# One graph layer on one core: the per-group sum of edge messages over two ranges of 16 nodes instead of one range of 32

## The chip, the core and the metric

The kernel runs on one core of a Trainium2 chip. The metric is the device time in microseconds, from one launch. PE is the matrix engine and PEld its loading of stationary operands, DVE the vector engine, ACT the scalar engine, POOL the engine that here issues the indirect gathers, and SP the engine that issues most other DMAs.

## What is computed

The layer takes 12,500 nodes of 160 features and 412,500 edges sorted by their target node `dst`. Cut to what matters:

```python
h = relu(layernorm(x))                       # 12500 x 160
l0, l1 = linear(h)                           # table of 160 columns, read by edge source
w = relu(edge_attr_10 @ W_fc1 * c) @ W_fc2   # 412500 x 192: w0 w1 (64 each), w2 w3 (32 each)
y0, y1 = l0[src], l1[src]
m0 = w0 * y0 * e0
m1 = (w1 * y0)[:, :, None] * e1[:, None, :]
m2 = (w2 * e0)[:, :, None] * y1
m3 = w3 * einsum('eud,ed->eu', y1, e1)       # times 1/sqrt(3)
s  = segment_sum(m, dst)                     # per node
out = x + second_linear(h, s)
```

The four edge attributes e0 and e1 multiply products of w and y, and the sum runs over all edges of a node.

## The kernel before

First the layer norm and the first linear map are computed for all nodes and written to DRAM as a table `T` (rows of 160 floats). Then the edge loop runs over NG = 538 groups `g` of six tiles `t` of 128 edges, and the last group has one tile. Each engine has its own program over all groups, and semaphores alone tie them together. A semaphore wait on an engine holds everything behind it on that engine.

For each group, by line of the kernel before:

- POOL (L525 to L533) gathers the 128 table rows of each tile into `Y`, with one `indirect_dma_start` per tile, six in a group. `Y` has NB = 4 buffers, so the gathers of group g + 4 wait until the last product of group g has been made (L527, semaphore `s_p`).
- PE `radial` (L662) makes the first edge layer, two matmuls of 384 columns into `bank[0]` and `bank[1]`. ACT `relu` (L586) moves it to `hs`. PE `weights(g, u)` (L672) makes w for the two tiles of unit u, with u = 0, 1, 2, into `bank[2]` or `bank[3]` in turn.
- DVE `windows` (L618 to L625) makes from the target numbers a table of zeros and ones `oh` over 32 nodes, and from it and the four edge attributes the stationary operand `S` (128 edges by 4 x 32 columns per tile). It also makes `Cm`, which shifts the previous group's sums. DVE `weigh(g, u)` (L633, L636) multiplies w with the gathered rows into `P`, two products s = 0, 1 of 160 columns for each edge, and raises `s_p`.
- PE `sums(g, u)` (L688) adds tile by tile into `bank[5 + g % 2]`: for each tile four matmuls of 32 stationary columns by 160 columns, one for each edge attribute k, in four column groups of the array. Attribute 0 takes the first product and attributes 1 to 3 the second.
- After the last unit four matmuls with one stationary column each (L695) add the row that group g shares with the previous group, from its finished sums `E` (the nodes at a boundary get edges from both). They raise `s_o`.
- ACT `evac_sum` (L593) copies the bank to `E` (three buffers) and raises `s_e`. SP `store` (L557) writes E to 32 rows of `s_sums` in DRAM at the group's first node, one store after the other (`s_out`), since neighbouring ranges overlap and the later one has the full row.

The order on PE is written out by hand: in group g come `sums(g, 0)`, `weights(g + 1, 0)`, `sums(g, 1)`, `weights(g + 1, 1)`, `sums(g, 2)` with the four small matmuls, `weights(g + 1, 2)`, and `radial(g + 2)`. `weights` with running number n waits for the product n - 2 (its bank is free then) and for `hs`. The order on ACT is `evac_sum(g)`, `relu(g + 2)`; on DVE it is `windows(g)` and three times `weigh`. `windows(g)` waits for `s_o` of group g - 2. Every five or six groups one tile of 128 finished nodes is read back and put through the second linear map, in steps between the groups (`load_sums`, `norm`, `turn_four`, `turn_last`, `second`, `residual`, `store_rows`).

A flag computed in the first stage tells whether the sorted targets fit the ranges. Otherwise a slow general loop runs.

## Time and profile before

| | us |
|---|---|
| median of 3 runs (lowest, highest) | 5671.61 (5670.48, 5678.02) |
| the profiled execution | 5666.25 |
| its span, first to last instruction | 5662.2 |
| PE, PEld, DVE, ACT, POOL busy | 4902.3, 2841.4, 2332.6, 752.3, 3099.8 |

The profiled execution is 4 us longer than its span, which is launch and end. Busy time is the time in which at least one instruction of the engine is under way by the records. The first 182 us of the span are the table, the last 30 us the last node tiles, and the edge loop fills the rest.

### The profile page before, as it was taken

The numbers are of one execution on the slowest core, as the hardware profiler recorded it, in microseconds if no ns is written. First come the engines' busy times: TensorE is split into PE (matmuls) and PEld (weight loads), VectorE is DVE, ScalarE is ACT, GpSimd is POOL, SyncE is SP. The second block draws the span as 40 slices with busy tenths as digits, with TensorE's granted clock in tenths as the row PEclk, the third lists the DMA queues.
The fourth block names the chain that finished last, engine by engine and source line by source line (L and its number), as shares of the span: only waits on it lengthen the run. The fifth ranks groups of instructions, "written<-read, shape, count | busy, mean of one in ns | idle before, by whom it ended". The sixth has DMA issues, their size and how long they took to land.

```text
span 5662.2 us, 102335 instructions
## 1 busy us (share of the span) xinstructions
PE 4902.3 (87%) x40750; PEld 2841.4 (50%) x40750; DVE 2332.6 (41%) x6909; ACT 752.3 (13%) x2130; POOL 3099.8 (55%) x3265
## 2 busy tenths in 40 slices
PE   8788888888888888888888888888888988888888
PEld 6445554444554445444455445444554555554454
DVE  5244444444444444444444444444444444444443
ACT  4111111111111111111111111111111111111111
POOL 1455555555555555555555555555555555555553
PEclk9877878888888888888878887888788778888888
DMA  4222222222222222222222222222222222222222
GB/s 134 66 71 71 72 71 73 70 71 72 72 71 72 73 73 71 73 71 73 71 73 71 72 72 73 73 70 73 71 73 70 73 73 71 73 71 73 73 70 61
DMA packets 378795, 412.92 MB, mean 73 GB/s; under 512 B 133782, under 2 KB 313269, under 8 KB 378063
## 3 DMA queue, kind: packets, MB, share of 16 engines
q0 software_dynamic: 155008, 265.17, 17.6%
q1 hardware_dynamic: 222831, 140.96, 9.0%
q8 instruction: 331, 5.42, 0.4%
q14 instruction: 145, 1.19, 0.1%
q10 hardware_dynamic: 480, 0.19, 0.0%
HBM read 345.79 MB, written 60.24 MB: 72 GB/s over the span
## 4 chain that ended last, share of the span: by engine, by line
another core or an unknown queue 80%; ACT 8%; PE 7%; issue 5%; DMA 0%; DVE 0%; ACTq 0%; SPq 0%
ACT hs L586 5%; PE bank L672 2%; PE bank L688 1%; ACT E L593 1%; PE bank L288 1%; ACT zt L449 1%; PE bank L286 1%; ACT zz L435 1%; PE bank L275 1%; PE bank L662 1%; PE bank L463 0%; PE bank L276 0%; ACT zt L457 0%; PE bank L695 0%
## 5 line engine op out<-in xcount | busy, mean ns | idle before, releaser
L530 POOL DMA_INDIRECT R<-l_table,src x3223 | 3070.0, 953 | 2388.0 <-DVE R L636 1546.9
L688 PE MATMUL bank<-R 128*32 128x160 f32 x25784 | 1998.4, 368 | 531.2 <-issue 525.5
L633 DVE TENSOR_TENSOR R<-bank,R 128x256 f32<-128x256 f32 x1612 | 680.8, 422 | 3208.1 <-remote 2045.7
L672 PE MATMUL bank<-w,hs 100*128 100x192 f32 x6446 | 1895.8, 427 | 72.6 <-ACT hs L586 34.5
L688 PEld LDWEIGHTS bank<-R 128*32 128x32 f32 x25784 | 910.7, 126 | 1506.1 <-issue 1405.8
L672 PEld LDWEIGHTS bank<-w,hs 100*128 100x128 f32 x6446 | 1303.8, 237 | 674.9 <-issue 405.2
L636 DVE TENSOR_TENSOR R<-bank,R 128x192 f32<-128x192 f32 x3224 | 984.9, 347 | 0.0
L593 ACT ACTIVATE E<-bank 128x160 f32<-128x160 f32 x538 | 163.2, 303 | 4764.2 <-remote 4708.3
L662 PE MATMUL bank<-ea,w1s 10*100 10x384 f32 x2152 | 598.8, 528 | 15.5 <-issue 12.9
L622 DVE TENSOR_TENSOR R<-bank,e 128x768 f32<-128x768 f32 x538 | 509.9, 948 | 0.0
L586 ACT ACTIVATE hs<-bank 100x384 f32<-100x384 f32 x1076 | 465.0, 488 | 21.0 <-PE bank L662 10.4
L695 PE MATMUL bank<-E,Cm 128*1 128x160 f32 x4296 | 283.7, 334 | 8.8 <-issue 8.6
L662 PEld LDWEIGHTS bank<-ea,w1s 10*100 10x100 f32 x2152 | 170.3, 164 | 211.3 <-issue 208.8
L463 PE MATMUL bank<-pw,zt 128*128 128x160 f32 (+1 forms) x980 | 205.2, 329 | 68.5 <-issue 65.6
L463 PEld LDWEIGHTS bank<-pw,zt 128*128 128x128 f32 (+1 forms) x980 | 150.3, 196 | 157.8 <-issue 154.9
L618 DVE TENSOR_TENSOR bank<-bank,rel 128x192 f32<-128x192 f32 x538 | 191.4, 356 | 4.2 <-DMA e<-in_e_t 4.2
L695 PEld LDWEIGHTS bank<-E,Cm 128*1 128x1 f32 x4296 | 124.1, 95 | 55.1 <-issue 12.6
L620 DVE TENSOR_SCALAR Cm<-dmat,dlt 128x4 f32<-128x4 f32 x538 | 143.2, 266 | 0.0
L444 PE MATMUL bank<-ident,zz 128*128 128x128 f32 x392 | 77.1, 295 | 38.7 <-issue 30.1
L233 POOL TENSOR_SCALAR hp<-x,mv 128x160 f32<-128x160 f32 x32 | 26.2, 819 | 130.1 <-PE bank L276 121.7
L444 PEld LDWEIGHTS bank<-ident,zz 128*128 128x128 f32 x392 | 43.9, 143 | 96.7 <-issue 88.5
L286 PE MATMUL bank<-bla,hta 128*128 128x128 f32 x196 | 62.8, 424 | 1.9 <-DVE hta L262 1.9
(77 smaller groups left out, 697.1 us busy)
## 6 DMA issues: line engine op xcount, KB each, us to landing
R<-l_table,src POOLq DMA_INDIRECT x3223
s_sums<-E SPq DMA_DIRECT2D x538, 80.0 KB
ea<-in_ea_p SPq DMA_DIRECT2D x269, 144.0 KB
x<-in_xp SPq DMA_DIRECT2D x14, 560.0 KB, 7.2
l_table<-ls SPq DMA_DIRECT2D x14, 560.0 KB, 3.3
zz<-s_sums SPq DMA_DIRECT2D x98, 80.0 KB
out<-os SPq DMA_DIRECT2D x98, 80.0 KB
e<-in_e_t SPq DMA_DIRECT2D x67, 96.0 KB
```

What stands on the lines that cost most here:

```text
L463: m = PE.matmul(bank[7][:, 0:C], zt[0:n, q, :], pw[0:n, q, :], start=q == 0, stop=q == 4)
L530: PL.indirect_dma_start(out=Y[:, g % NB, t, :], out_offset=None, in_=T, in_offset=bass.IndirectOffsetOnAxis(ap=src[:, k:k + 1], axis=0),). ...
L586: AC.activation(hs[:, g % 2, i * 384:(i + 1) * 384], bank[i][0:100, 0:384], ACT.Relu, scale=REL).then_inc(s_hs, 1)
L593: AC.activation(E[:, g % 3, :], bank[5 + g % 2][:, 0:C], ACT.Copy).then_inc(s_e, 1)
L618: V.tensor_tensor(oh[:, g % 2, :, :], steps.unsqueeze(1).to_broadcast([128, G, WIN]), rel[:, g, :].unsqueeze(2).to_broadcast([128, G, WIN] ...
L622: V.tensor_tensor(S[:, g % 2, :, :].rearrange("p t (k n) -> p t k n", k=4), oh[:, g % 2, :, :].unsqueeze(2).to_broadcast([128, G, 4, WIN]) ...
L633: V.tensor_tensor(p[:, :, :, 0:64], w[:, :, 0:128].rearrange("p t (s c) -> p t s c", s=2), y[:, :, 0:64].unsqueeze(2).to_broadcast([128, n ...
L636: m = V.tensor_tensor(p[:, :, s, 64:160].rearrange("p t (d c) -> p t d c", d=3), w[:, :, 128 + 32 * s:160 + 32 * s].unsqueeze(2).to_broadc ...
L662: PE.matmul(bank[i][0:100, 0:384], w1s[r, :], ea[r, g // 2 % 3, o:o + 384], start=True, stop=True).then_inc(s_h, 1)
L672: m = PE.matmul(bank[2 + n % 2][:, o * 192:(o + 1) * 192], hs[:, g % 2, t * 128:(t + 1) * 128], w2[:, :], start=True, stop=True, skip_grou ...
L688: m = PE.matmul(b[q, 0:C], S[:, g % 2, t, q], P[:, g % 2, t, o:o + C], start=t == 0, stop=t == tiles(g) - 1)
L695: m = PE.matmul(b[32 * k:32 * k + 1, 0:C], Cm[:, g % 2, k:k + 1], E[:, (g - 1) % 3, :], start=False, stop=True, skip_group_check=True)
```

## The change

The range of 32 nodes per group becomes two ranges of 16 nodes, one for every 384 edges (`HALF`). The tiles of a group are dealt out again: tile 2u + h is the u-th tile of half h, so each unit has one tile of either half. `S` has for each tile 64 columns, 16 nodes by 4 attributes with the attribute innermost. One matmul per tile multiplies them with all 320 columns of `P`. Half 0 goes to partitions 0 to 63 of the bank and half 1 to 64 to 127. So each attribute is summed against both products, of which one is used. `E` and `s_sums` are twice as wide (320 columns per node and attribute).

The carry between neighbouring ranges, four matmuls of one column in a group before, becomes two matmuls of four stationary columns by 320, one for each half: `carry(g, 0)` takes half 1 of group g - 1, and `carry(g, 1)` takes half 0 of group g. The second can only run when ACT has copied half 0, so PE runs it in the next group, behind `weights(g + 2, 0)` (in the loop: `carry(g - 1, 1)` after unit 0). ACT copies the halves apart (`evac_sum(g, 0)`, `relu(g + 2)`, `evac_sum(g, 1)`), SP stores them apart, 80 KB each, and all waits on `s_o`, `s_e` and `s_out` count two in a group.

```diff
-WIN = 32
+WIN = 16
+HALF = 3 * 128
...
-    A = nc.dram_tensor("s_sums", [NP, 4, C], f32).ap()
+    A = nc.dram_tensor("s_sums", [NP, 4, 2 * C], f32).ap()
...
-            def store(g):
-                b = SP.value_load(bas[0:1, 0, g:g + 1])
+            def store(g, h):
+                n = 2 * g + h
+                b = SP.value_load(bas[0:1, n:n + 1])
                 b = SP.snap(b, min_val=0, max_val=NP - WIN)
-                SP.wait_ge(s_e, g + 1)
-                if g:
-                    SP.wait_ge(s_out, 16 * g)
-                SP.dma_start(A[bass.ds(b, WIN), :, :].rearrange("n k c -> k n c"), E[:, g % 3, :]).then_inc(s_out, 16)
+                SP.wait_ge(s_e, n + 1)
+                if n:
+                    SP.wait_ge(s_out, 16 * n)
+                SP.dma_start(A[bass.ds(b, WIN), :, :].rearrange("n k c -> (n k) c"), E[64 * h:64 * h + 64, g % 3, :]
+                             ).then_inc(s_out, 16)
...
             for g in range(NG):
-                evac_sum(g)
+                evac_sum(g, 0)
                 relu(g + 2)
+                if halves(g) > 1:
+                    evac_sum(g, 1)
...
                 if g >= 2:
-                    V.wait_ge(s_o, g - 1)
+                    V.wait_ge(s_o, 2 * g - 2)
...
-                for t in range(2 * u, min(2 * u + 2, tiles(g))):
-                    for k in range(4):
-                        q = slice(32 * k, 32 * k + 32)
-                        o = 0 if k == 0 else C
-                        m = PE.matmul(b[q, 0:C], S[:, g % 2, t, q], P[:, g % 2, t, o:o + C], start=t == 0,
-                                      stop=t == tiles(g) - 1)
-                if last:
-                    if g:
-
-                        PE.wait_ge(s_e, g)
-                        for k in range(4):
-                            m = PE.matmul(b[32 * k:32 * k + 1, 0:C], Cm[:, g % 2, k:k + 1], E[:, (g - 1) % 3, :],
-                                          start=False, stop=True, skip_group_check=True)
+                for t in parts(g, u):
+                    h = t % 2
+                    m = PE.matmul(b[64 * h:64 * h + 64, 0:2 * C], S[:, g % 2, t, :], P[:, g % 2, t, :], start=u == 0,
+                                  stop=not (u + 1 < 3 and t + 2 in parts(g, u + 1)))
+                if g == 0 and u == units(g)[-1]:
                     m.then_inc(s_o, 1)
+
+            def carry(g, h):
+
+                f = 64 * (1 - h)
+                PE.wait_ge(s_e, 2 * g + h)
+                PE.matmul(bank[5 + g % 2][64 * h:64 * h + 4, 0:2 * C], Cm[f:f + 64, g % 2, :],
+                          E[f:f + 64, (g - 1 + h) % 3, :], start=False, stop=True, skip_group_check=True).then_inc(s_o, 1)
...
                     if g + 1 < NG and u in units(g + 1):
                         weights(g + 1, u)
+                    if u == 0 and g:
+                        carry(g - 1, 1)
+                if g:
+                    carry(g, 0)
                 if g + 2 < NG:
                     radial(g + 2)
```

On PE, one group of the steady loop, before (L688 `sums`, L672 `weights`, L695 the four small matmuls, L662 `radial`; a form is stationary columns by moving columns):

```order
L688 MATMUL bank<-R 32x160 [waits s_p,s_e,s_S]
L688 MATMUL bank<-R 32x160 x7
L672 MATMUL bank<-w,hs 128x192 [waits s_p,s_hs]
L672 MATMUL bank<-w,hs 128x192
L688 MATMUL bank<-R 32x160 [waits s_p]
L688 MATMUL bank<-R 32x160 x7
L672 MATMUL bank<-w,hs 128x192 [waits s_p,s_hs]
L672 MATMUL bank<-w,hs 128x192
L688 MATMUL bank<-R 32x160 [waits s_p]
L688 MATMUL bank<-R 32x160 x7
L695 MATMUL bank<-E,Cm 1x160 [waits s_e]
L695 MATMUL bank<-E,Cm 1x160 x3
```

The same place in the changed kernel (L710 `sums`, L697 `weights`, L719 `carry`):

```order
L710 MATMUL bank<-R 64x320 [waits s_p,s_e,s_S]
L710 MATMUL bank<-R 64x320
L697 MATMUL bank<-w,hs 128x192 [waits s_p,s_hs]
L697 MATMUL bank<-w,hs 128x192
L719 MATMUL bank<-E,Cm 4x320 [waits s_e]
L710 MATMUL bank<-R 64x320 [waits s_p]
L710 MATMUL bank<-R 64x320
L697 MATMUL bank<-w,hs 128x192 [waits s_p,s_hs]
L697 MATMUL bank<-w,hs 128x192
L710 MATMUL bank<-R 64x320 [waits s_p]
L710 MATMUL bank<-R 64x320
L697 MATMUL bank<-w,hs 128x192 [waits s_p,s_hs]
```

Eight matmuls in a unit have become two, and one carry now stands behind the first `weights`.

On ACT in the same part of the program, before:

```order
L593 ACTIVATE E<-bank 128x160 [waits s_out,s_o]
L586 ACTIVATE hs<-bank 100x384 [waits s_h,s_wp]
L586 ACTIVATE hs<-bank 100x384 [waits s_h]
L593 ACTIVATE E<-bank 128x160 [waits s_out,s_o]
L586 ACTIVATE hs<-bank 100x384 [waits s_h,s_wp]
```

And in the changed kernel:

```order
L615 ACTIVATE E<-bank 64x320 [waits s_out,s_o] x2
L607 ACTIVATE hs<-bank 100x384 [waits s_h,s_wp]
L607 ACTIVATE hs<-bank 100x384 [waits s_h]
L615 ACTIVATE E<-bank 64x320 [waits s_out,s_o] x2
L607 ACTIVATE hs<-bank 100x384 [waits s_h,s_wp]
```

The copy of half 1 of a group and that of half 0 of the next stand one behind the other, and both stand ahead of the next `relu`.

## Rows read from the trace of the kernel before

**Rows 1.** The page: busy time by engine, and the chain by engine.

```profile
PE 4902.3 (87%) x40750; PEld 2841.4 (50%) x40750; DVE 2332.6 (41%) x6909; ACT 752.3 (13%) x2130; POOL 3099.8 (55%) x3265
...
another core or an unknown queue 80%; ACT 8%; PE 7%; issue 5%; DMA 0%; DVE 0%; ACTq 0%; SPq 0%
```

**Rows 2.** Waits, 300 to 5500 us: waiter, releaser; us in total, times, longest.

```profile
POOL R L530 <- DVE R L636: 1484.7, 513, 4.1
```

**Rows 3.** PE timeline, last groups, no gathers: start, length, line, count, [idle before].

```profile
5622.77 0.75 PE L688 MATMUL bank<-R 128*32 128x160 f32 x16
5623.48 0.92 PE L672 MATMUL bank<-w,hs 100*128 100x192 f32 x4
5624.32 0.75 PE L688 MATMUL bank<-R 128*32 128x160 f32 x16
...
5628.47 0.75 PE L688 MATMUL bank<-R 128*32 128x160 f32 x16
```

**Rows 4.** Windows: stretch, length, busy us (instructions) by engine, PEclk, DMA share, GB/s.

```profile
300.00:5500.00 5200.00, 4522.22 (x38341) 2591.40 (x38336) 2142.79 (x6250) 644.83 (x1817) 2933.09 (x3080) 0.81 0.27 72
```

**Rows 5.** POOL timeline: one group's gathers, and the first of the next.

```profile
3004.72 0.95 POOL L530 DMA_INDIRECT R<-l_table,src  x1 [2.97 <-DVE R L636]
3005.97 0.95 POOL L530 DMA_INDIRECT R<-l_table,src  x1 [0.30 <-issue]
...
3011.01 0.95 POOL L530 DMA_INDIRECT R<-l_table,src  x1 [0.30 <-issue]
3014.86 0.95 POOL L530 DMA_INDIRECT R<-l_table,src  x1 [2.90 <-DVE R L636]
```

**Rows 6.** PE timeline of the same group.

```profile
3007.05 0.92 PE L672 MATMUL bank<-w,hs 100*128 100x192 f32 x4
...
3008.46 0.46 PE L695 MATMUL bank<-E,Cm 128*1 128x160 f32 x8
3008.84 0.92 PE L672 MATMUL bank<-w,hs 100*128 100x192 f32 x4
3009.83 0.48 PE L662 MATMUL bank<-ea,w1s 10*100 10x384 f32 x1
3010.54 0.90 PE L662 MATMUL bank<-ea,w1s 10*100 10x384 f32 x3 [0.24 <-issue]
```

**Rows 7.** DVE timeline of the same group.

```profile
3010.58 0.42 DVE L633 TENSOR_TENSOR R<-bank,R 128x256 f32<-128x256 f32 x1 [3.60 <-PE bank L672]
...
3013.64 0.42 DVE L633 TENSOR_TENSOR R<-bank,R 128x256 f32<-128x256 f32 x1 [2.11 <-remote]
3013.98 0.61 DVE L636 TENSOR_TENSOR R<-bank,R 128x192 f32<-128x192 f32 x2
```

**Rows 8.** ACT timeline of the same group.

```profile
3013.58 0.30 ACT L593 ACTIVATE E<-bank 128x160 f32<-128x160 f32 x1 [8.68 <-remote]
```

**Rows 9.** Windows of that group and of the first groups; columns as in Rows 4.

```profile
3004.70:3010.50 5.80, 5.54 (x53) 3.33 (x52) 2.03 (x6) 0.20 (x1) 4.56 (x5) 0.81 0.50 124
3013.40:3014.80 1.40, 1.40 (x14) 0.90 (x14) 1.16 (x5) 1.06 (x3) 0.00 (x0) 0.64 0.00 0
182.44:198.80 16.36, 13.86 (x67) 7.33 (x65) 5.39 (x15) 1.74 (x4) 12.52 (x13) 0.79 0.37 87
198.80:224.00 25.20, 6.22 (x18) 2.15 (x18) 0.95 (x3) 0.00 (x0) 16.19 (x17) 0.55 0.22 59
```

**Rows 10.** Groups by shape, 300 to 5500 us: busy us, mean ns of one.

```profile
L622 DVE TENSOR_TENSOR R<-bank,e 128x768 f32<-128x768 f32 x513 | 486.2, 948 | 0.0
L586 ACT ACTIVATE hs<-bank 100x384 f32<-100x384 f32 x1026 | 443.4, 488 | 4.0 <-PE bank L662 3.5
...
L618 DVE TENSOR_TENSOR bank<-bank,rel 128x192 f32<-128x192 f32 x513 | 182.5, 356 | 0.0
...
L593 ACT ACTIVATE E<-bank 128x160 f32<-128x160 f32 x513 | 155.6, 303 | 4550.0 <-remote 4540.6 <-PE bank L695 9.4
```

**Rows 11.** SP timeline, the last two stores, the second waiting for the first.

```profile
5638.07 3.53 SPq L557 DMA_DIRECT2D s_sums<-E  x2
```

More of the change, by code:

```diff
@@ L567, in build @@
                     load_e4(g // EC + 1)
-                store(g)
+                for h in range(halves(g)):
+                    store(g, h)
                 if g % 2:
@@ L646, in build @@
                 windows(g)
-                V.wait_ge(s_y[g % NB], 16 * G * (g // NB) + 16 * tiles(g))
+                V.wait_ge(s_y[g % NB], 16 * G * (g // NB) + 16 * count(g))
                 for u in units(g):
@@ L677, in sums @@
                 b = bank[5 + g % 2]
-                last = u == units(g)[-1]
                 if u == 0:
@@ L720, in build @@
                     second(j)
+            if halves(NG - 1) > 1:
+                carry(NG - 1, 1)
             finish(lambda j, d: ready[j] + d >= NG)
```

140 lines of the change are left out of this document (79 added, 61 removed).

## Prediction, made before the changed kernel was run

> **What bounds the kernel now.** I read the page's busy times first, then its chain, then the last groups of the loop, and then one group in the middle, engine by engine.
>
> The busy times alone mislead [rows 1]. PE is busy 87% of the span, so fewer or shorter matmuls look like the lever. But the chain gives PE 7% and an unknown cause 80%. The last groups say what PE needs when nothing else disturbs it. There POOL has issued its last gather, and the same PE work comes round every 5.70 us (5622.77 to 5628.47, no gap) [rows 3]. In the steady loop a group takes 5200/513 = 10.14 us [rows 2, 4]. So 4.4 us per group are not PE's work, and the difference between the stretches is that gathers run.
>
> The middle group shows how they cost time. POOL's six calls start 1.26 us apart (3004.72 to 3011.01 is five steps, 6.29 us) [rows 5]. While their transfers are in flight, PE's matmuls start on time, but the engines that wait for them are not released on time. The second `weights` is done by its own record at 3007.97, and DVE, idle for it, starts its product at 3010.58. The four small matmuls are done at 3008.92, and ACT copies the sums at 3013.58 [rows 6 to 8]. Then everything comes free at once: ACT at 3013.58, DVE at 3013.64. That is when the gathers' transfers have ended: the DMA share is 0.00 from 3013.40 on [rows 9]. DVE makes the last product (to 3014.59), which frees a buffer of `Y`, and POOL starts the next six at 3014.86 [rows 5, 7]. So the loop closes: 6.29 (six calls) + 2.57 (last call to the release) + 0.06 + 0.95 (product) + 0.27 (POOL) = 10.14 us. PE's array time is not a term of it.
>
> How much PE gets through while gathers fly can be counted [rows 9]. From the first call (3004.70) to 3010.50 it started 53 + 52 = 105 instructions, and then stood. Of these the ones behind the second `weights` were not yet reported: 32 of `sums`, 16 small, 8 `weights`, 2 to 4 `radial`, some 60. So about 45 were reported in 5.8 us. At the start of the loop, where gathers run without a break, PE started 132 instructions in 16.4 us and then only 36 in 25.2 us: **0.70 us for each instruction**, whatever it is. My reading is a store of reports that holds some 37 (45 less 5.8/0.70) and empties at one per 0.70 us while gathers are in flight, and at once when they are over. PE is then fast for some 37 instructions after POOL starts and stands after that, with some 60 more begun.
>
> **The change part by part.**
> *PE instructions.* A group has 144 records before (48 + 12 + 4 + 8 matmuls, and as many loads). After it has 12 + 12 + 4 + 4 = 32 matmuls and 32 loads, 64. By themselves these 80 fewer are worth nothing as long as the loop above closes in the same way.
>
> *Array time of `sums`.* Before, 16 records of 160 columns run four abreast, 0.71 us from the unit's start to the next [rows 3]. After, 4 records of 320 columns run two abreast, if the two halves of the array are independent: the same time. If they are not, a unit takes up to 0.71 us more. No row shows 64 columns; I take zero. The Trainium skill (TensorEngine Tiling (Array Packing), Available Configurations) lists 128x64 as two independent tiles, which would make it zero, against 0.71.
>
> *Carries.* Before, 8 records four abreast take 0.38 us (3008.46 to 3008.84) [rows 6]. After, 4 records of twice the columns come one by one: with 0.71/4 = 0.18 us for a step of 160 columns at most 4 x 0.36 = 1.4, so +1.0 at most. PE's own need goes from 5.70 to some 6.7 us, still under 10. It costs 4 x 0.8 = +3 us in the last four groups, where PE alone sets the time.
>
> *DVE.* `windows` shrinks: 384 elements instead of 768 and 96 instead of 192. By (948 - 356)/576 = 1.03 ns per element these take 0.55 and 0.26 us [rows 10], and with `Cm` the three take about 1.0 instead of 1.4. DVE is idle before its products, so this saves nothing in the loop above.
>
> *ACT.* By (488 - 303)/224 = 0.83 ns per column a copy of 320 columns takes 0.44 us, two of them in place of one of 0.30 [rows 10]. ACT is busy 13%. Behind it wait `relu` and with it the first `weights`, 0.13 us later, covered by the gathers.
>
> *Stores.* Two of 80 KB instead of one. One after another they go every 3.53 - 0.6 = 2.9 us [rows 11], so two fit in 5.9 of 10 us. 8 GB/s are added to 72 and the DMA share is 0.27 [rows 4]: I take zero. `load_sums` stands behind the second store on SP, and its reader comes two groups later.
>
> *The new wait.* `windows(g)` on DVE now waits for the carry of half 1 of group g - 2, which PE runs behind `weights(g, 0)`. Before, it waited for sums that were all reported at the release. Queued behind it on DVE are all three products of group g, and behind the last of them POOL.
>
> *Putting it together.* From the release to the report of the last `weights` of the next group PE must now report 8 + 4 + 8 + 8 + 8 + 8 = 44 instructions. 37 + 5/0.70 = 44 are let through 5 us after POOL's start, so before its six calls (7.5 us) are over. POOL then finds its buffer free and goes on without a break. That saves the 2.57 + 0.06 + 0.95 + 0.27 us once. But the second group is then at one report per 0.70 us: the carry and `radial` need 12 reports, then `relu`, then 8 more, some 15 us, while the second six calls and their landing take 10. So the release comes with the end of the second six, and at that point only the first `weights` of the next group is ready. The carry of which `windows` is waiting came with it. From there to POOL's start: `windows` 1.0, product 0.95, the third `weights`, which waits for that product, 0.84/0.81 = 1.04 (its step in the last groups [rows 3], at the mean clock [rows 4]), product 0.95, POOL 0.27: **4.21 us**. Two groups cost 11 x 1.258 + 2.57 + 4.21 = 20.62 us, 10.31 each instead of 10.14. At about 530 groups that is +90 us. With the last groups' +3 and some 4 us less at the start, where PE stands for 25 us: against the profiled span 5662 + 89 = 5751, with 4 us of launch 5755. The profiled execution was 5 us below the median, so on the median's scale it is **5760**. If `weights` runs at half the clock in that stretch, 2 x 0.84 instead of 1.04, the 4.21 becomes 4.85, a group 10.63, and the time 5930.
>
> **The rivals.**
> *A, the loop stays closed.* If fewer than 44 reports get through in time (37 + 7.5/0.70 = 48 is a thin margin), each group still ends with its own release: 10.14, and 5672 + 3 - 4 = **5671**. For it: the loop has no term that the change touches, and POOL's wait in front of its calls hardly varies (1484.7/513 = 2.9 us in the mean, 4.1 at most [rows 2]), though every fifth group has a node tile's matmuls more. Chance 0.18.
>
> *B, more groups per release.* If the 0.70 us belong to the many small matmuls, or the store of reports is larger than I count (85 or more), three groups go through: (17 x 1.258 + 2.57 + 4.21)/3 = 9.39 us, -0.75 x 530: **5275**. For it: the 36 slow instructions at the start were mostly `sums`. Against it: `weights` among them were as slow. Chance 0.20.
>
> *C, POOL alone is the bound.* If the release no longer hangs on gathers, a group takes six calls, 7.55 us: 5672 - 2.59 x 530 = **4300**. Nothing in the rows shows PE at speed for long beside gathers, so its chance is 0.06. The Trainium skill (SBUF — State Buffer, SBUF: two separate sides) says that engine ports and DMA ports are apart, so that neither slows the other; by it PE would not wait for gathers, and the loop would be at this bound before the change too. Here 5.70 against 10.14 us speak against it.
>
> *D, the new wait decides each time.* If the carry for `windows` is reported only with the release also in a cycle of one group, that cycle is 6.29 + 2.57 + 4.21 = 13.07 us. Mixed with cycles of two it gives (13.07 + 20.62)/3 = 11.2 us, **6250**. It decides when fewer than 12 reports get through after the first `weights` starts; 37 do. If the two column halves do not run side by side, two units of `sums` in the 4.21 add 1.4, and the time is 6040. Together 0.12.
>
> *That the ranges do not fit* (the general loop would run, far slower): in the drawn inputs 384 consecutive edges never span more than 15 nodes, so 16 hold. Left out.
>
> **How the numbers follow.** My forecast, cycles of mostly two groups, 5700 to 5930, has 0.44. A has 0.18, B 0.20, C 0.06, D 0.12. The range goes from B to just over my own upper bound, 5270 to 5950; outside lie C, D. About 0.2% (11 us) is what a measurement here can tell from no change. Faster: B, C and a part of A (the start) = 0.29. Same: the rest of A = 0.15. Slower: 0.44 + 0.12 = 0.56.
>
> **What would show it.** POOL's idle time in front of its gathers tells most. Right: every second group starts without a gap, and the others after 6 to 7 us. A: 2.9 us before each group, as now. B: two of three without a gap. D: over 5 us before each. The records of `sums` must start in pairs a few ns apart; in single file means D. DVE's `windows` should start right after the release in the long gaps; where it does not, the new wait is not what is late. PE's last groups should take 6.5 to 6.7 us. The prediction is wrong at its root if PE reports on time beside gathers, or if the slow stretch at the start of the loop has gone.

## The result, and the profile after

The changed kernel takes **6094.75 us** (median of 4, 6064.63 to 6142.73) against 5672.15 us (median of 4) before: a ratio of 1.0751, 95% interval 1.0676 to 1.0826. The forecast was 5760 us, and its range ended at 5950. It is slower, as forecast, but by almost five times as much. Two kernels below (`a_split4` and `a_sum160`) had one run each that was over 1.5% slower than their fastest, and their times are the medians of the others.

The page after, in the order of [rows 1]: busy time by engine, the chain by engine and by line, and the costliest PE groups (busy us, mean ns of one).

```profile
PE 5457.3 (90%) x19264; PEld 2425.1 (40%) x19264; DVE 2049.5 (34%) x6919; ACT 1133.7 (19%) x2667; POOL 3109.8 (51%) x3265
...
PE 74%; another core or an unknown queue 16%; issue 5%; DVE 3%; ACT 1%; DMA 0%; ACTq 0%; SPq 0%; DVEq 0%
PE bank L697 26%; PE bank L710 19%; PE bank L719 13%; PE bank L687 8%; PE bank L472 3%; DVE R L661 1%; PE bank L453 1%; DVE R L658 1%; ACT hs L607 1%; PE bank L292 1%; PE bank L290 1%; PE bank L279 1%; PE bank L462 0%; DVE bank L643 0%
...
L710 PE MATMUL bank<-R 128*64 128x320 f32 x6446 | 1645.9, 599 | 0.0
...
L719 PE MATMUL bank<-E,Cm 64*4 64x320 f32 x2148 | 988.9, 549 | 0.5 <-ACT E L615 0.5
```

PE executes less than half as many matmul records (19264 for 40750) and is busy for 555 us more. Its part of the chain goes from 7% to 74%: the loop is no longer closed by late reports alone; PE's own work is in it. L719 are the two new carries, 989 us of busy time where the eight small records before had 284.

Windows tell when. They give the stretch, its length, busy us (instructions) of PE, PEld, DVE, ACT and POOL, the granted clock, the DMA share and GB/s. After, first the loop as a whole, then five groups at half clock, then two at full clock:

```profile
300.00:5900.00 5600.00, 5059.10 (x17927) 2197.37 (x17925) 1884.89 (x6295) 1015.41 (x2344) 2962.25 (x3101) 0.72 0.29 74
2925.89:2989.19 63.30, 63.30 (x167) 25.35 (x169) 18.11 (x60) 10.07 (x24) 28.68 (x30) 0.50 0.24 62
...
5867.51:5884.98 17.47, 16.28 (x85) 7.90 (x83) 7.06 (x24) 5.20 (x12) 11.46 (x12) 1.00 0.32 84
```

The same views of the kernel before, one group each, at half and at full clock:

```profile
4412.57:4422.69 10.12, 10.12 (x73) 5.54 (x71) 4.13 (x14) 1.50 (x5) 5.72 (x6) 0.50 0.28 73
...
5405.33:5415.45 10.12, 8.37 (x84) 5.36 (x83) 4.03 (x14) 1.28 (x4) 5.73 (x6) 1.00 0.27 73
```

In these stretches a group takes 10.12 us before, at either clock. After, it takes 17.47/2 = 8.74 us at full clock (2.4 GHz) and at half clock (1.2 GHz) 63.30/5 = **12.66 us**, and there PE has no pause: 63.30 us busy of 63.30. The change is a gain at full clock and a larger loss at half clock, and the granted clock of the loop fell from 0.81 [rows 4] to 0.72.

All groups can be sorted in this way, by the starts of POOL's gathers and the trace's records of the granted clock. A group is put under a clock if it has it for 99% of its time:

| kernel | groups | mean us | wholly full clock | wholly half clock | the rest |
|---|---|---|---|---|---|
| before | 527 | 10.13 | 26: 10.10 | 4: 10.12 | 497: 10.13 |
| after | 527 | 10.87 | 143: 9.16 | 131: 12.71 | 253: 10.88 |

Against 10.13 us a group, those at half clock cost 131 x 2.58 = +338 us, those at full clock -143 x 0.97 = -139, the rest 253 x 0.75 = +190: together +389 of the 398 us between the two profiled spans.

The steps of PE at half clock, in the first of those five groups (PE timeline, start and length):

```profile
2925.72 1.60 PE L687 MATMUL bank<-ea,w1s 10*100 10x384 f32 x4
2927.25 1.33 PE L710 MATMUL bank<-R 128*64 128x320 f32 x4
2928.52 1.65 PE L697 MATMUL bank<-w,hs 100*128 100x192 f32 x4
2930.10 1.23 PE L719 MATMUL bank<-E,Cm 64*4 64x320 f32 x2
2931.25 1.33 PE L710 MATMUL bank<-R 128*64 128x320 f32 x4
...
2938.10 1.60 PE L687 MATMUL bank<-ea,w1s 10*100 10x384 f32 x4
```

From `radial` to `radial` 12.38 us, without idle time. The groups of the tail, where [rows 3] has 5.70 us, take at full clock

```profile
6018.23 0.76 PE L710 MATMUL bank<-R 128*64 128x320 f32 x4
6018.93 0.92 PE L697 MATMUL bank<-w,hs 100*128 100x192 f32 x4
6019.78 0.70 PE L719 MATMUL bank<-E,Cm 64*4 64x320 f32 x2
...
6024.93 0.76 PE L710 MATMUL bank<-R 128*64 128x320 f32 x4
```

6.70 us, as forecast. Before, the half-clock group of 4413 us steps through the same pieces in 10.48 us (its PE timeline; `weights` 1.58 us three times, `sums` 1.22, 1.22 and 1.07, small matmuls 0.69, `radial` 1.54):

```profile
4413.61 1.29 PE L688 MATMUL bank<-R 128*32 128x160 f32 x16
4414.83 1.65 PE L672 MATMUL bank<-w,hs 100*128 100x192 f32 x4
4416.41 1.30 PE L688 MATMUL bank<-R 128*32 128x160 f32 x16
4417.48 0.76 PE L695 MATMUL bank<-E,Cm 128*1 128x160 f32 x8
4418.17 1.65 PE L672 MATMUL bank<-w,hs 100*128 100x192 f32 x4
4419.75 1.60 PE L662 MATMUL bank<-ea,w1s 10*100 10x384 f32 x4
```

So the kernel before stood at the edge. At half clock PE needed 10.48 us where the loop gave it 10.12. My reading is that it fell a little behind and made it up at full clock, since its stretches at half clock are short (7 us in the mean, see below) and its groups wholly at half clock still take 10.12. Whatever is added to its array time counts double there, and has no cover.

Where the half clock begins shows in the stretch before those five groups (all engines, cut):

```profile
2913.62 0.70 PE L719 MATMUL bank<-E,Cm 64*4 64x320 f32 x2
...
2915.79 0.76 PE L710 MATMUL bank<-R 128*64 128x320 f32 x4
...
2919.41 0.96 POOL L548 DMA_INDIRECT R<-l_table,src  x1 [0.30 <-issue]
2921.15 0.43 ACT L615 ACTIVATE E<-bank 64x320 f32<-64x320 f32 x1 [9.59 <-remote]
2921.16 0.27 DVE L643 TENSOR_TENSOR bank<-bank,rel 128x96 f32<-128x96 f32 x1 [6.00 <-remote]
...
2923.02 1.62 PE L697 MATMUL bank<-w,hs 100*128 100x192 f32 x4 [6.47 <-DVE R L661]
```

PE's carry ended at 2914.32 and its `sums` at 2916.55. ACT and DVE, which wait for the carry, went on only at 2921.15, 1.7 us after POOL's last call. PE stood for 6.47 us (the clock records have the fall in this pause, at 2919.59), came back at half clock and kept it for over 60 us of work without a pause.

POOL's gaps, the sign that the prediction named (POOL timeline, idle time before each call in brackets):

```profile
5423.38 0.95 POOL L548 DMA_INDIRECT R<-l_table,src  x1 [2.87 <-DVE R L661]
...
5432.56 0.95 POOL L548 DMA_INDIRECT R<-l_table,src  x1 [1.92 <-DVE R L661]
...
5440.14 0.96 POOL L548 DMA_INDIRECT R<-l_table,src  x1 [0.30 <-issue]
...
5452.19 0.95 POOL L548 DMA_INDIRECT R<-l_table,src  x1 [4.78 <-DVE R L661]
```

A group without a gap does occur (5440.14), but 58 times among 527, not every second time. Groups take from 7.54 to 15.34 us, where those of before take from 9.80 to 11.29.

### The profile page after: what moved, and what is told of

It reads as the page before. It is cut to its first block, busy times and chain, and to the rows that moved or that the text cites. A ratio compares the mean times of both kernels' runs of the same rounds, so it can differ in the third digit from the quotient of the medians.

```text
span 6060.7 us, 63130 instructions
## 1 busy us (share of the span) xinstructions
PE 5457.3 (90%) x19264; PEld 2425.1 (40%) x19264; DVE 2049.5 (34%) x6919; ACT 1133.7 (19%) x2667; POOL 3109.8 (51%) x3265
## 4 chain that ended last, share of the span: by engine, by line
PE 74%; another core or an unknown queue 16%; issue 5%; DVE 3%; ACT 1%; DMA 0%; ACTq 0%; SPq 0%; DVEq 0%
PE bank L697 26%; PE bank L710 19%; PE bank L719 13%; PE bank L687 8%; PE bank L472 3%; DVE R L661 1%; PE bank L453 1%; DVE R L658 1%; ACT hs L607 1%; PE bank L292 1%; PE bank L290 1%; PE bank L279 1%; PE bank L462 0%; DVE bank L643 0%
## 5 line engine op out<-in xcount | busy, mean ns | idle before, releaser
L697 PE MATMUL bank<-w,hs 100*128 100x192 f32 x6446 | 1990.7, 446 | 568.4 <-DVE R L661 284.8
L697 PEld LDWEIGHTS bank<-w,hs 100*128 100x128 f32 x6446 | 1370.3, 248 | 1721.5 <-issue 1290.8
L710 PE MATMUL bank<-R 128*64 128x320 f32 x6446 | 1645.9, 599 | 0.0
L615 ACT ACTIVATE E<-bank 64x320 f32<-64x320 f32 x1075 | 464.1, 432 | 4414.2 <-PE bank L719 2699.1
L719 PE MATMUL bank<-E,Cm 64*4 64x320 f32 x2148 | 988.9, 549 | 0.5 <-ACT E L615 0.5
L643 DVE TENSOR_TENSOR bank<-bank,rel 128x96 f32<-128x96 f32 x538 | 143.5, 267 | 2250.1 <-PE bank L719 983.8
L710 PEld LDWEIGHTS bank<-R 128*64 128x64 f32 x6446 | 392.4, 167 | 841.8 <-issue 836.4
L687 PE MATMUL bank<-ea,w1s 10*100 10x384 f32 x2152 | 650.4, 690 | 0.6 <-ACT hs L607 0.6
L647 DVE TENSOR_TENSOR R<-bank,e 128x384 f32<-128x384 f32 x538 | 298.6, 555 | 0.0
L719 PEld LDWEIGHTS bank<-E,Cm 64*4 64x4 f32 x2148 | 93.6, 80 | 334.2 <-issue 332.6
```

The source lines that it names most:

```text
L615: AC.activation(E[64 * h:64 * h + 64, g % 3, :], bank[5 + g % 2][64 * h:64 * h + 64, 0:2 * C], ACT.Copy).then_inc(s_e, 1)
L647: V.tensor_tensor(S[:, g % 2, :, :].rearrange("p t (n k) -> p t n k", k=4), oh[:, g % 2, :, :].unsqueeze(3).to_broadcast([128, G, WIN, 4]) ...
L687: PE.matmul(bank[i][0:100, 0:384], w1s[r, :], ea[r, g // 2 % 3, o:o + 384], start=True, stop=True).then_inc(s_h, 1)
L697: m = PE.matmul(bank[2 + n % 2][:, o * 192:(o + 1) * 192], hs[:, g % 2, t * 128:(t + 1) * 128], w2[:, :], start=True, stop=True, skip_grou ...
L710: m = PE.matmul(b[64 * h:64 * h + 64, 0:2 * C], S[:, g % 2, t, :], P[:, g % 2, t, :], start=u == 0, stop=not (u + 1 < 3 and t + 2 in parts ...
L719: PE.matmul(bank[5 + g % 2][64 * h:64 * h + 4, 0:2 * C], Cm[f:f + 64, g % 2, :], E[f:f + 64, (g - 1 + h) % 3, :], start=False, stop=True, ...
```

## The experiments

Each batch had its own chip, with the kernel before timed beside it. In the first three batches before took 5671, 5669 and 5726 us; in the last two 4271 and 4273 us, and those are told apart at the end.

Each run has a label: it starts with `a` for an edit of the changed kernel and with `b` for one of the kernel before.

**Is it the wait that was added?** The changed kernel, windows released by the sums themselves, with a third buffer for `Cm` (`a_early`):

```diff
-                if g >= 2:
-                    V.wait_ge(s_o, 2 * g - 2)
+                if g == 2:
+                    V.wait_ge(s_o, 1)
+                if g > 2:
+                    V.wait_ge(s_q, g - 2)
...
-                if g == 0 and u == units(g)[-1]:
-                    m.then_inc(s_o, 1)
+                if u == units(g)[-1]:
+                    m.then_inc(s_o if g == 0 else s_q, 1)
```

> The changed kernel, with the wait of windows(g) put back on the sums of group g - 2 (a semaphore of its own behind the last sums matmul) and three buffers for Cm, so that DVE no longer waits for the carry that PE runs one group later. Theory W (the new wait is what costs): PE's pauses ahead of weights go, and the time returns to 5680 to 5800 us. Theory T (the array time decides: PE needs 6.7 us a group at the full clock and 13.4 at half, more than the 10.14 of the gather loop): the wait is beside the point and the time stays at 6050 to 6130.

6098.55 us, ratio 1.0763 (1.0745 to 1.0782): nothing changed. The waits of DVE (us in total, times, longest), first in the changed kernel for the carry, then with the edit for `weights`:

```profile
DVE bank L643 <- PE bank L719: 953.1, 292, 7.5
```

```profile
DVE R L661 <- PE bank L700: 1793.9, 909, 9.8
```

The wait that was added only stood where the next one stands without it. It is not the cause. (The edit touches DVE's wait alone: ACT still waits for the carry before each copy of the sums, and `relu` stands behind these copies.)

**Is it the carries' array time?** The changed kernel, both carries on 32 of 320 columns (the rest of each straddling node's sum is left out, `a_small`):

```diff
-                PE.matmul(bank[5 + g % 2][64 * h:64 * h + 4, 0:2 * C], Cm[f:f + 64, g % 2, :],
-                          E[f:f + 64, (g - 1 + h) % 3, :], start=False, stop=True, skip_group_check=True).then_inc(s_o, 1)
+                PE.matmul(bank[5 + g % 2][64 * h:64 * h + 4, 0:32], Cm[f:f + 64, g % 2, :],
+                          E[f:f + 64, (g - 1 + h) % 3, 0:32], start=False, stop=True, skip_group_check=True).then_inc(s_o, 1)
```

> The changed kernel with both carries cut to 32 of 320 columns, same order, same waits (the carry of the other 288 columns is left out). PE's own need falls from 6.7 to about 5.8 us a group at the full clock. Theory T: most of the loss goes, 5670 to 5800 us. Theory W: the wait is as late as before, 6000 to 6100.

5851.62 us, ratio 1.0332 (1.0308 to 1.0357). That is 243 of the 423 us, 57%. Nine of its groups at half clock:

```profile
2773.54:2872.78 99.24, 99.24 (x308) 48.18 (x306) 33.01 (x109) 18.29 (x42) 51.57 (x54) 0.50 0.30 75
```

99.24/9 = 11.03 us where the changed kernel has 12.66, again without a pause of PE. Full-clock groups fell to 8.01 (74 of them). But the clock fell too, to 0.65 in the loop, which took back a part of the gain.

What is left, 179 us, is not array time. PE's own group takes 5.74 us in the tail of this kernel, where the kernel before has 5.70, and 10.46 us at half clock, from `radial` to `radial`, where that one has 10.48:

```profile
2782.20 1.60 PE L687 MATMUL bank<-ea,w1s 10*100 10x384 f32 x4
...
2792.66 1.60 PE L687 MATMUL bank<-ea,w1s 10*100 10x384 f32 x4
```

Counted as in the table above, 229 groups wholly at half clock cost 229 x 0.76 = +174 us against 10.13, 74 at full clock give back 74 x 2.12 = 157, and the other 224 cost 224 x 0.56 = +125. Before, 4 groups were wholly at half clock. With the same array time it is the longer stretches at half clock that cost here.

**And the other way round, does array time count in the kernel before?** Two matmuls of four rows by 320 columns are added ahead of the four small ones; their result is not used (`b_pad`):

```diff
+                        for h in range(2):
+                            PE.matmul(b[0:4, 160:480], ident[0:64, 0:4], x[0:64, 0:2, :], start=True, stop=True,
+                                      skip_group_check=True)
                         PE.wait_ge(s_e, g)
```

> The kernel before with two matmuls more in each group, of the form of the changed kernel's carries (64 rows, 4 stationary columns, 320 moving columns, into bank columns that nothing reads), ahead of the four small ones: some 1.1 us of array time a group at the full clock and 8 instructions. Theory T (array time costs by itself, also before): slower by some of 538 x 1.1, up to 6200 us. Theory L (before the change the loop is closed by the gathers, and PE's array time is not in it): 5670 to 5720.

6029.76 us, ratio 1.0652 (1.0615 to 1.0689). Three groups at half clock, two at full clock:

```profile
4979.25:5017.87 38.62, 38.62 (x225) 18.49 (x217) 12.22 (x36) 3.93 (x11) 17.16 (x18) 0.50 0.22 55
...
5070.49:5091.50 21.01, 17.10 (x171) 8.81 (x172) 8.96 (x27) 2.45 (x7) 11.44 (x12) 1.00 0.27 67
```

Over all groups: 50 at half clock with 12.12 us (before: 10.12), 26 at full clock with 10.29 (before: 10.10), 451 between with 10.58 (10.13). Two such matmuls take about as long as two carries (a step of 0.63 us each in the tail above): 1.16 us at full clock in the tail of this kernel, and 2.22 at half clock. Put on a kernel whose loop was said to have no term of it, they cost 360 us, and groups wholly at full clock take only 0.19 us more. The mean clock hardly moved (0.80 for 0.81), so the loss does not need a lower clock; by these groups it needs stretches at half clock in which PE can't finish a group in 10.1 us.

**What do the fewer instructions give?** First the changed kernel with each matmul of `sums` cut into four of 80 columns (same columns in all, 36 matmul records and 36 weight loads more a group; the sums it makes are not those of the layer, so it measures time alone; `a_split4`):

```diff
-                for t in parts(g, u):
-                    h = t % 2
-                    m = PE.matmul(b[64 * h:64 * h + 64, 0:2 * C], S[:, g % 2, t, :], P[:, g % 2, t, :], start=u == 0,
-                                  stop=not (u + 1 < 3 and t + 2 in parts(g, u + 1)))
+                for c in range(0, 2 * C, 80):
+                    for t in parts(g, u):
+                        h = t % 2
+                        m = PE.matmul(b[64 * h:64 * h + 64, c:c + 80], S[:, g % 2, t, :], P[:, g % 2, t, c:c + 80],
+                                      start=u == 0, stop=not (u + 1 < 3 and t + 2 in parts(g, u + 1)),
+                                      skip_group_check=True)
```

> The changed kernel with each sums matmul of 320 columns cut into four of 80: the array time is the same, and PE's instructions go from 64 to 136 a group (before: 144). Theory I (with few instructions PE's reports do not run into the bound beside gathers, the groups overlap in another way and PE drops to the low clock): like before the change, some 5700 to 5800. Theory T (array time alone): 6090, as the changed kernel.

6465.84 us, ratio 1.1463 (1.1385 to 1.1541). The array time is the same (a group of the tail takes 6.73 us, for 6.70), but its full-clock groups take 10.23 us (26 of them), as in the kernel before; the gain of the changed kernel at full clock, 9.16, is gone. So that gain came from the count. These 72 instructions a group cost 371 us. By an estimate from that, the 8 which `b_pad` adds (4 matmul records and 4 loads) cost some 40 of its 360 us, so the count doesn't explain that run. Then the kernel before without attributes 1 to 3 of tiles 1 to 4, whose matmuls ran beside those of attribute 0 (`b_k0`):

```diff
-                    for k in range(4):
+                    for k in range(1 if 0 < t < tiles(g) - 1 else 4):
```

> The kernel before, with the sums of edge attributes 1 to 3 left out for tiles 1 to 4 of each group (tiles 0 and 5 stay whole); 12 of 24 sums matmuls go. Those left out ran side by side with the one that stays, so the time in the array is the same and only the number of instructions and the columns streamed side by side fall. Theory N (array time and number of instructions): 12 matmuls fewer a group are a gain, by the 375 us for 72 of the column split about 60 us: 5610 us, mean clock 0.82 as before. Theory K (the clock follows what is streamed side by side): half-clock stretches grow from a mean of 7 us to 15 us or more, the mean clock falls to about 0.72, and the time is 5750 us or more.

5581.82 us, ratio 0.9754 (0.9732 to 0.9775), with full-clock groups of 8.67 us (32) and half-clock groups of 10.56 (20). Leaving out these 24 matmul records and 24 loads is worth 2.5%, at a clock of 0.77 for 0.81; the matmuls that stay take as long in the array as all took before (a group of the tail takes 5.66 us, for 5.70).

**Why is the clock lower after?** Two tries. In the changed kernel only 160 of 320 columns in the second and third unit of `sums` (half of their columns is left out, `a_sum160`; `HW(u)` is 320 for u = 0 and 160 otherwise):

```diff
-                    m = PE.matmul(b[64 * h:64 * h + 64, 0:2 * C], S[:, g % 2, t, :], P[:, g % 2, t, :], start=u == 0,
+                    m = PE.matmul(b[64 * h:64 * h + 64, 0:HW(u)], S[:, g % 2, t, :], P[:, g % 2, t, 0:HW(u)], start=u == 0,
```

> The changed kernel with the sums matmuls of units 1 and 2 cut to 160 of 320 columns (the second product of four of six tiles is left out): PE's own need falls by 2 x 0.27 = 0.5 us in the streaming of these units, by about 0.55 us a group at the full clock and 1.1 at half. Theory T: by the carries' figure (240 us back for some 1.0 us) 130 to 250 us less, 5850 to 5970. Theory I: little change, 6050 to 6100.

6230.26 us, ratio 1.0989 (1.0971 to 1.1007), at a mean clock of 0.58 to 0.60, where the changed kernel has 0.72: less work and slower. With the lower clock of `a_small` this suggested that the columns streamed side by side keep the clock up. The test of it, the sums in matmuls of 32 stationary columns, four abreast in place of two (`a_quad`):

```diff
-                    m = PE.matmul(b[64 * h:64 * h + 64, 0:2 * C], S[:, g % 2, t, :], P[:, g % 2, t, :], start=u == 0,
-                                  stop=not (u + 1 < 3 and t + 2 in parts(g, u + 1)))
+                    for q in (0, 32):
+                        m = PE.matmul(b[64 * h + q:64 * h + q + 32, 0:2 * C], S[:, g % 2, t, q:q + 32],
+                                      P[:, g % 2, t, :], start=u == 0,
+                                      stop=not (u + 1 < 3 and t + 2 in parts(g, u + 1)))
```

> The changed kernel with each of the six sums matmuls of a group cut in two by its 64 stationary columns: two matmuls of 32 columns by 320, so that four stand side by side where two did. The time in the array per group stays, the columns that are streamed while it works double, and a group has 6 matmuls (12 records) more. Theory K (the clock: what is streamed side by side decides how long the engine stays at half clock): the half-clock stretches get shorter, from a mean of 22 us towards the 7 us of the kernel before, the mean granted clock rises from 0.72 to about 0.80, and the time falls to 5750 to 5950 us. Theory N (only array time and the number of instructions count): the 4-way column split cost 375 us for 72 more matmuls a group, so 6 more cost about 30 us: 6120 us, clock 0.72.

6149.45 us beside 5725.81, ratio 1.0717 (1.0661 to 1.0774), which can't be told from the change itself, and the same share of time at half clock, 57% (the changed kernel has 56%). The idea falls. The gain at full clock is gone here too, with 24 instructions more a group: 116 groups wholly at full clock take 10.09 us. (The expectations of this run and of `b_k0` took the 72 instructions of `a_split4` for 72 matmuls; they are 18 matmuls, so the cost that they put on each matmul was too small by a factor of four.) The loop of this kernel:

```profile
300.00:5900.00 5600.00, 5004.17 (x23602) 2078.38 (x23601) 1843.19 (x6150) 992.51 (x2293) 2888.32 (x3033) 0.71 0.30 73
```

What is left is a description. By the clock records between 300 and 5300 us, half-clock stretches last 7 us in the mean before (264 of them) and 22 us after (126). The falls come after idle time of PE: the 5 us ahead of a fall hold 2.45 us of it in the mean after and 1.27 before, where any 5 us of the loop hold 0.48 and 0.65. Pauses of PE of over 2 us are 0 before and 101 after. Without gathers, and so without pauses, the loop is at full clock throughout (below). But such pauses alone don't make the stretches long: `b_k0` has 203 of them, and its stretches last 8 us. Why PE's dense work stays at half clock for 60 us in one place and 7 us in another stays open. So does whether the new order makes the pauses: that ACT's copies wait for a carry which PE runs later, and `relu` behind them, was not taken away in any run.

**The stores' bytes.** The changed kernel stores and reads back only 160 of 320 columns of each node and attribute (`a_halfstore`):

```diff
-                SP.dma_start(A[bass.ds(b, WIN), :, :].rearrange("n k c -> (n k) c"), E[64 * h:64 * h + 64, g % 3, :]
+                SP.dma_start(A[bass.ds(b, WIN), :, 0:C].rearrange("n k c -> (n k) c"), E[64 * h:64 * h + 64, g % 3, 0:C]
...
```

> The changed kernel with only the first 160 of 320 columns of each node range written to memory (and read back later), which is what the later steps use for attribute 0 and wrong for the others: the bytes of each store halve, 64 pieces of 640 B instead of 1280 B, two stores a group as before. If the stores' transfers or their contention with the gathers carry the loss: 100 us or more faster than 6095 us. If they don't: 6095 us within 0.5%.

6229.21 us, ratio 1.0869 (1.0847 to 1.0891). Halving the bytes gains nothing. The ratio is even higher than the changed kernel's, which wasn't timed on this chip, with more groups wholly at half clock (166 for 131) of the same 12.71 us. The bytes, which are here those of the kernel before, are not the cause. That a group has two stores instead of one was not tested.

**What would each kernel take without gathers?** Both with gathers for the first four groups only; all later products use those rows (the edit of the changed kernel, `a_nogather`; that of the kernel before, `b_nogather`, is the same at its own lines):

```diff
                 if g >= NB:
-                    PL.wait_ge(s_p, 3 * (g - NB + 1))
+                    break
...
-                V.wait_ge(s_y[g % NB], 16 * G * (g // NB) + 16 * count(g))
+                if g < NB:
+                    V.wait_ge(s_y[g % NB], 16 * G)
```

> The changed kernel with the gathers of the first four groups only; all later groups use these rows (all other gathers are left out). If gathers in flight are what holds PE's reports back, a group takes 6.7 us, PE's own need at the full clock as in the last groups of the trace, and the time is 210 + 538 x 6.7, about 3820 us. If the changed PE program by itself keeps the clock low, up to 7000.

> The kernel before with the gathers of the first four groups only (the others are left out). PE's own need is 5.70 us a group in its last groups, so 210 + 538 x 5.8, about 3330 us. The changed kernel took 4070 without gathers, so the change should cost some 700 us here, all of it array time.

The changed kernel 4070.27 us (ratio 0.7177, 0.7162 to 0.7192), the kernel before 3524.53 us (one run). Windows, changed kernel first:

```profile
300.00:3900.00 3600.00, 3599.56 (x17533) 1634.25 (x17532) 1818.99 (x6151) 1002.52 (x2295) 0.00 (x0) 1.00 0.18 44
```

```profile
300.00:3300.00 3000.00, 2999.77 (x36632) 1925.97 (x36625) 2046.73 (x5972) 669.46 (x1736) 0.00 (x0) 1.00 0.15 39
```

PE is dense and at full clock throughout. By PE's matmuls per us against those of the loop with gathers (17927 in 5600 us at 10.87 us a group; 38341 in 5200 at 10.13), a group takes 7.15 us after and 6.12 us before, node tiles and all: the change adds 1.03 us of PE work a group. The forecast had said at most +1.0.

**A better order for the kernel before.** Its four small matmuls move behind the first `weights` of the next group, and `relu` ahead of the copy of the sums (`b_late`):

```diff
-                evac_sum(g)
                 relu(g + 2)
+                evac_sum(g)
...
+                    if u == 0 and g > 1:
+                        carry(g - 1)
```

> The kernel before, with its four small matmuls moved behind the first weights of the next group and ACT's copy behind relu, so that windows(g) waits for a carry that PE runs later, as in the changed kernel; nothing else changes and the array time is that of before. Theory W: slower, 5800 to 6100 us. Theory T: 5670, as before.

5574.58 us, ratio **0.9824** (0.9808 to 0.9841), with nothing left out. Neither theory of the expectation had it faster. Groups take 9.96 us, at full clock 10.00 and at half clock 9.80. Its waits (us in total, times, longest), to be held against [rows 2]:

```profile
POOL R L530 <- DVE R L636: 1390.5, 512, 3.8
...
ACT E L593 <- PE bank L696: 821.2, 506, 5.8
DVE bank L618 <- PE bank L696: 794.3, 506, 4.0
```

POOL's wait falls by 0.18 us a group, which is all of the gain (527 x 0.18 = 95 us, of 97). With the windows besides released by the sums, as in the first experiment (`b_late_early`):

> The kernel before with its four small matmuls moved behind the first weights of the next group and the relu placed ahead of the copy (as in b_late), and besides with the windows of group g waiting for the sums of group g-2 on a semaphore of their own instead of for its small matmuls, with three buffers for the small matmuls' stationary. If the wait of VectorE for the small matmuls is late anywhere in b_late: 20 to 80 us faster than 5575 us. If VectorE has slack there, as in the changed kernel, where the same edit moved nothing: 5575 us within 0.3%.

5643.09 us beside 5725.81, ratio 0.9867 (0.9848 to 0.9886): no further gain. Which of the two moves in the order brings the 1.8% was not separated.

**The other kind of chip.** To test the loop itself, both kernels and the better order got a fifth buffer for gathered rows, an edit of one constant (`a_nb5`, `b_nb5`, `b_late_nb5`):

```diff
-    NB = 4
+    NB = 5
```

> The changed kernel with five buffers for the gathered rows instead of four, so that GpSimd waits for the release of group g-5 and not g-4. Theory H (full-clock groups are set by the loop of gathers, 9.2 us, half-clock groups by TensorE's own work at half clock, 12.6 us): a fifth buffer shortens only the first kind and the pauses of TensorE; half-clock groups stay at 12.0 to 12.6 us, and the time falls only by what full-clock groups and a higher mean clock give: 5700 to 5950 us. Rival L (everything is the loop: 10.87 us a group at four buffers): the same loop over five buffers is 8.7 us a group, with no difference between half and full clock: about 4900 us. Rival F (the gathers themselves can't come faster beside this work): 6095 us within 0.5%.

> The kernel before with five buffers for the gathered rows instead of four. If the loop of gathers closed over four buffers set its 10.13 us a group: the same loop over five gives 8.1 us where TensorE is at full clock, and at half clock TensorE's own work, just under 10.1 us, holds: with half of the groups each, about 9.1 us a group and 5110 us. If the loop's length grows with the groups that are ahead (each report is late by a time per instruction that stands ahead of it, not per buffer): 5670 us within 0.5%.

> The order of b_late (four small matmuls behind the first weights of the next group, relu ahead of the copy) with five buffers for the gathered rows. If both gains are of the same kind (time in the loop of gathers): as b_nb5 within 0.5%. If they are apart: b_nb5 times 0.98.

On this chip the kernel before, untouched, takes 4271.09 us (21 runs, 4270.35 to 4273.73), a quarter less than on the others. The three kernels take 4278.46, 4271.42 and 4273.69 us, ratios 1.0024, 1.0001 and 1.0006. The batch was repeated beside the changed kernel itself (`after2`) and met a second chip of that kind:

> The changed kernel as it is, once more, beside before on the same chip. In the batch before this one the kernel before took 4271 us on its chip, with a gather every 1.26 us and no gap, where four other chips gave 5669 to 5726 us. If the chip here is of the second kind: 1.075 times before, as in the first measurement. If it is of the kind that gave 4271 us: the gathers' 7.54 us a group bound both kernels, TensorE needs 6.7 us at full clock, and the ratio is 0.99 to 1.03.

> The changed kernel with five buffers for gathered rows, once more. On a chip where before takes 5670 us or more: by theory H (full-clock groups set by the loop, half-clock groups by TensorE's work) 5700 to 5950 us; by rival L (all is loop) about 4900 us; by rival F 1.075 times before. On a chip where before takes 4271 us: 4278 us again.

> The kernel before with five buffers for gathered rows, once more. On a chip where before takes 5670 us or more: about 5110 us if the loop over four buffers sets its 10.13 us, 5670 us within 0.5% if each report is late by what stands ahead of it. On a chip where before takes 4271 us: 4271 us again.

Before 4272.90 us; the change 4304.75 us, ratio **1.0077** (1.0060 to 1.0094); with five buffers 4280.69 and 4272.99 us, ratios 1.0023 and 1.0000. The changed kernel's page and its POOL timeline there:

```profile
PE 4176.5 (97%) x19264; PEld 1939.7 (45%) x19264; DVE 2043.4 (48%) x6919; ACT 1141.9 (27%) x2667; POOL 3100.3 (72%) x3265
...
PE 46%; POOL 39%; issue 13%; DMA 1%; DVE 1%; ACT 0%; SPq 0%; ACTq 0%; DVEq 0%; POOLq 0%
```

```profile
202.88 0.95 POOL L548 DMA_INDIRECT R<-l_table,src  x1 [0.30 <-issue]
204.14 0.95 POOL L548 DMA_INDIRECT R<-l_table,src  x1 [0.30 <-issue]
205.39 0.95 POOL L548 DMA_INDIRECT R<-l_table,src  x1 [0.30 <-issue]
```

POOL issues a gather every 1.26 us and hardly ever waits, 7.54 us a group. The window in which [rows 9] counts 0.70 us for each PE instruction, first in the changed kernel on the chip of the first measurement, then on this one:

```profile
198.80:224.00 25.20, 7.58 (x22) 3.29 (x20) 1.91 (x6) 0.00 (x0) 16.91 (x18) 0.50 0.24 62
```

```profile
198.80:224.00 25.20, 25.20 (x68) 10.84 (x66) 8.20 (x27) 3.46 (x8) 19.05 (x21) 0.50 0.31 77
```

42 instructions in 25.2 us on the one, 0.60 us each, and 134 on the other, where PE is busy throughout at the same half clock. PE isn't held up there, with 21 gathers issued in that time for 18. In a group of the loop PE's 7.15 us at full clock then lie just under POOL's 7.54, which fits that the change costs 0.8% there and not 7.5%; where the 0.8% are lost wasn't looked into. What sets the two kinds of chip apart no run shows. Since no batch with five buffers met a chip of the first kind, what a fifth buffer does there wasn't measured.

## Why the prediction was wrong, by its steps

*The loop before, 10.14 us, "PE's array time is not a term of it".* **This step failed.** It nearly holds at full clock, where 1.2 us more array time cost 0.19 us (`b_pad`). At half clock PE needed 10.48 us for its own steps and had 10.12. There array time decides: 12.12 us with the pad, 12.71 after the change, PE busy without a pause in the stretches shown. The rows with the clock could have told: [rows 9] has 0.81 for one stretch and 0.64 for the next, and [rows 4] a mean of 0.81, which is full clock for 62% of the time and half clock for 38%, never 0.81.

*"Still under 10".* PE's need was forecast as 6.7 us at full clock, and 6.70 was measured; `sums` ran in pairs side by side, as forecast (4 records of 320 columns in 0.76 us). The error is in the comparison. At half clock the 6.7 us are 12.4, over 10. The half clock was looked at for one `weights` (the 5930), not for the whole group.

*44 reports, so every second group without a gap.* The theory of late reports was right that fewer instructions help at full clock: groups there take 9.16 instead of 10.10, `b_k0` gains, `a_split4` loses that gain. Its store of 37 reports was not tested by any run. The pattern was not right: 58 gapless groups of 527. The sum of 10.31 has one array term, a `weights` of 1.04 us at the mean clock; by the rows the groups wholly at one clock take 9.16 and 12.71 us, and neither is near it.

*Part by part.* DVE's windows take 267 and 555 ns (forecast 0.26 and 0.55 us), ACT's copy 432 ns (0.44), the last groups 6.70 us (6.7). Stores: taken as zero, and halving their bytes gained nothing. The new wait: priced in 4.21 us and in rival D; taking it away changed nothing (`a_early`). That the change would be slower was right in sign only: the forecast had it from this wait and gave 88 us, the runs have it from other causes and give 423.

*The rivals.* A (5671) stood on the same failed step. B's price (5275) was not reached anywhere. D gave 6250 for the new wait, near to the result, but its mechanism is refuted by `a_early`: nearly the right size for a wrong reason, which is luck. C, POOL alone as the bound, "4300", had 0.06 and is what two of the chips do, by the kernel before (4271 and 4273 us); the changed kernel itself was timed on one of them, 4304.75 us. The prediction called itself wrong at its root if PE reports on time beside gathers: on these chips it does. The Trainium skill (SBUF — State Buffer, SBUF: two separate sides) has engine ports and DMA ports apart. On those chips the trace agrees (134 PE instructions in 25.2 us beside gathers). On the chip of the first measurement 42 in the same time speak against it, though no run shows that SBUF ports are where it is disturbed.

*The cause, as far as shown.* On the chips of the first kind it is more array time per group, 57% of the loss in the two carries, paid where the clock is halved, and a larger share of such time. The first is shown by taking it away (`a_small`), by adding the like to the kernel before (`b_pad`), and by PE's rows without a pause. The second, from 38% to 56% of the loop, is measured but its cause stays open: neither the columns side by side nor the stores' bytes explain it. `a_small` had more of it (71%), with PE's need as before the change, and the 43% of the loss that stay in it are found in its groups with half clock. The order on ACT and PE, which all runs of the changed kernel kept, stands untested.

## What to carry to other kernels

Compare an engine's need with the loop at each clock that the trace grants it, not at the mean: a PE at 5.7 us of 10.1 looked idle for half of the time and had nothing left at half clock. When an edit halves the number of instructions but puts matmuls in single file that stood four abreast, price the array time twice, once at each clock. And a time from one chip may be of one kind only: the same change cost 7.5% on one and 0.8% on another.

## What the runs showed of the hardware that was not expected

- The same program took 5669 to 5726 us on three chips and 4271 and 4273 us on two others, each within 0.2% in itself. On the first kind, work that waits for PE can go on late while gathers are in flight (the carry done at 2914.32, ACT and DVE going on at 2921.15; 42 PE instructions in 25.2 us), on the second PE made 134 in the same window.
- PE can stay at half clock through over 60 us of work without a pause (63.30 us busy of 63.30), after an idle time of 6.47 us.
- Less work can be slower: `sums` with half of the columns in two of three units took 6230 us at a mean clock of 0.58 to 0.60, where the whole took 6095 at 0.72.
